# Two layers, Chebyshev attention beside an expert network: the attention output's transpose and projection move from the prefix sums' PSUM bank to a free quarter of the projection's bank

## What is computed

```python
xn = _layernorm(x, axis=-1)
qkv = jnp.einsum('bsd,ed->bse', xn, W_in)
xq = jnp.clip(q * inv_sqrt_d, -1.0 + EPS_CLAMP, 1.0 - EPS_CLAMP)
xk = jnp.clip(k * inv_sqrt_d, -1.0 + EPS_CLAMP, 1.0 - EPS_CLAMP)
Tq, Tk = _cheb(xq), _cheb(xk)                     # Chebyshev terms
kv_prefix = jnp.cumsum(Tk * v[:, :, :, None, :], axis=2)
ks_prefix = jnp.cumsum(Tk.sum(axis=-1), axis=2)
num = (Tq * kv_prefix * beta).sum(axis=3)
den = (Tq.sum(axis=-1) * ks_prefix * beta).sum(axis=3)
s = einsum(num / (den + EPS_DEN), W_out)
# beside it: a mixture of 8 experts, 2 per token
out = sum over e of cw_e * (gelu(xn @ w1[e].T + b1[e]) @ w2[e].T + b2[e])
x = x + s * silu(_layernorm(out + xn, ln_w, ln_b))
```

## Time and profile before

| what | value |
|---|---|
| median of 3 runs | 925.35 us (923.32 to 929.02) |
| profiled execution, its own time | 925.38 us |
| span in the profile | 923.5 us |
| mean granted TensorE clock | 0.849 of full |
| TensorE busy | 601.0 us (65%) |
| VectorE busy | 633.4 us (69%) |
| ScalarE busy | 449.1 us (49%) |
| GpSimd busy | 435.8 us (47%) |

### The profile page before, as it was taken

The page is one execution under the profiler, slowest core; times in us unless marked ns, Lnnn a source line. Parts: engine busy times, 40 slices in busy tenths (PEclk is TensorE's granted clock), DMA queues, the critical chain, the costliest instruction groups (busy, mean ns, idle before and its releaser), DMA issues.

```text
span 923.5 us, 21985 instructions
## 1 busy us (share of the span) xinstructions
PE 601.0 (65%) x7047; PEld 407.0 (44%) x7047; DVE 633.4 (69%) x1667; ACT 449.1 (49%) x1075; POOL 435.8 (47%) x697
## 2 busy tenths in 40 slices
PE   1888888888888888634542677667766776751220
PEld 0455555555555555422221455445544555520110
DVE  4587777777777777548671766776677667846667
ACT  1455555555555555313332676777677767610001
POOL 3145444444444444427774333333333333357783
PEclk9999999999999999856565888899889988955555
DMA  9910000000000000001113022222222222111221
GB/s 240 318 53 2 3 2 0 0 0 0 0 0 0 0 0 1 2 6 52 49 50 107 24 92 92 69 71 92 92 70 72 90 93 70 46 48 55 66 67 49
DMA packets 64526, 49.53 MB, mean 54 GB/s; under 512 B 10056, under 2 KB 55376, under 8 KB 64464
## 3 DMA queue, kind: packets, MB, share of 16 engines
q1 hardware_dynamic: 59328, 39.74, 13.8%
q0 software_dynamic: 5136, 9.02, 3.5%
HBM read 18.83 MB, written 18.35 MB: 40 GB/s over the span
## 4 chain that ended last, share of the span: by engine, by line
PE 34%; POOL 17%; issue 16%; ACT 15%; DVE 15%; DMA 2%; DVEq 1%; SPq 0%; POOLq 0%; ACTq 0%
POOL xbuf L528 7%; POOL experts_sb L541 7%; PE m_ps L986 6%; PE e_ps L998 5%; PE p_ps L869 4%; PE q_ps L899 2%; ACT xs L703 2%; PE y_ps L951 2%; ACT vd L603 2%; PE p_ps L943 2%; DVE x_all L1149 2%; ACT pexp L695 1%; DVE rot L1118 1%; ACT xs L608 1%; PE y_ps L832 1%
## 5 line engine op out<-in xcount | busy, mean ns | idle before, releaser
L576 ACT ACTIVATE pexp<-e_ps 128x512 f32<-128x512 f32 x128 | 76.4, 597 | 75.5 <-PE e_ps L816 73.8
L1260 DVE TENSOR_SCALAR early<-p_ps 128x256 f32<-128x256 f32 x32 | 13.6, 424 | 117.4 <-ACT vs L650 117.4
L986 PE MATMUL m_ps<-xs,wb 128*128 128x512 f16 x276 | 89.8, 442 | 2.1 <-ACT xs L703 1.3
L1085 DVE TENSOR_REDUCE mneg<-m_ps 128x4 bf16<-128x512 f32 x128 | 84.5, 681 | 4.6 <-PE m_ps L783 4.6
L528 POOL DMA_INDIRECT xbuf<-x,slots x64 | 65.9, 1030 | 33.6 <-issue 19.2
L958 PE MATMUL q_ps<-eye_sb,yn 128*128 128x128 f32 x32 | 11.5, 358 | 106.3 <-ACT early L671 75.5
L541 POOL DMA_INDIRECT experts_sb<-ybuf,slots x64 | 65.9, 1029 | 28.7 <-issue 18.5
L492 POOL COPY xs<-xs 128x128 f16<-128x128 f16 x32 | 12.8, 399 | 105.1 <-ACT xs L608 105.1
L603 ACT COPY vd<-p_ps 64x64 f32<-64x64 f32 x128 | 27.0, 211 | 71.8 <-DVE early L1120 69.4
L832 PE MATMUL y_ps<-pexp,vd 128*32 128x128 f32 x512 | 54.9, 283 | 2.8 <-ACT pexp L576 0.6
L1044 PE MATMUL e_ps<-b_sb,cwt 8*128 8x128 f32 x64 | 16.6, 436 | 61.7 <-ACT cwt L744 61.7
(11 more groups left out here) (218 smaller groups left out, 2124.2 us busy)
## 6 DMA issues: line engine op xcount, KB each, us to landing
wb<-experts_sb SPq DMA_DIRECT2D x46, 256.0 KB, 2.4
xbuf<-zero_sb SPq DMA_DIRECT2D x23, 256.0 KB, 4.0
xs<-xbuf SPq DMA_DIRECT2D x23, 256.0 KB, 2.9
ybuf<-rt SPq DMA_DIRECT2D x23, 256.0 KB, 2.5
experts_sb<-in_experts_w SPq DMA_DIRECT2D x8, 512.0 KB, 7.3
x_all<-in_x SPq DMA_DIRECT2D x8, 256.0 KB, 5.6
xbuf<-x,slots POOLq DMA_INDIRECT x64, 2.2
experts_sb<-ybuf,slots POOLq DMA_INDIRECT x64, 2.5
```

Source lines behind the costliest of these rows:

```text
L576: nc.scalar.activation(pexp[:, j, :, :], e_ps[j % 2][:, :, :], ACT.Exp, scale=float(D) ** -0.5).then_inc(exp_ready.sem, 1)
L986: last = nc.tensor.matmul(u_ps[f % 2], wb1[:, i % 2, f, a, :], xg16[:, i % 2, b, :], start=k == 0, stop=k == len(PARTS) - 1)
L1085: nc.vector.tensor_reduce(mneg[:, n.batch, j // 2, (j % 2) * NG:(j % 2) * NG + NG], m_ps[j % 2][:, :, :], AX.X, ALU.max, negate=True).then ...
```

## The change

`o_ps` becomes the fourth quarter of `p_ps`, the bank that `project` fills to three quarters. The waits follow the bank: the transpose no longer waits for the carry copies, but for the two readers of the projection (`v_copy` and `clip` of the chunk two ahead) and for the `s1_copy` of the chunk before; `sums` loses its wait on `s1_copy`, and `project` gets it. No instruction is added, removed or put elsewhere.

```diff
-        o_ps = cc_ps[1][:, 3 * P:4 * P]
+        o_ps = p_ps[:, 3 * C:4 * C]
...
                 after(pe, s_v_copied, c)
                 after(pe, s_clipped, c)
+                after(pe, s_s1_copied, c - 2)
                 nc.tensor.matmul(p_ps[:, 0:3 * C], xn1t_all[:, c, :], w_in[:, :], start=True, stop=True).then_inc(s_projected2, 1)
...
                 after(pe, s_carry_copied, min(c, NT - B))
-                after(pe, s_s1_copied, c)
                 nc.tensor.matmul(cc_ps[0][:, 0:3 * SW], tri_sb[:, :], kv[:, c % 2, 0:3 * SW], start=True, stop=True)
...
             def transpose_out(c):

                 pe.wait_ge(s_outs, CHEB2 * (c + 1))
-                pe.wait_ge(s_carry_copied, min(c + 1, NT - B))
+                pe.wait_ge(s_v_copied, min(c + 3, NT))
+                pe.wait_ge(s_clipped, min(c + 3, NT))
+                after(pe, s_s1_copied, c)
                 nc.tensor.transpose(o_ps, oc[:, :], eye_sb[:, :]).then_inc(s_oc_transposed, 1)
```

## The result

The changed kernel takes 883.57 us (median of 4 runs, 880.61 to 884.25) against 926.25 us of the kernel before (4 runs on the same chips, 923.32 to 929.02). The ratio is 0.9533, 95% interval 0.9496 to 0.9571: faster by 4.7%. The forecast was 883.0 us, range 871 to 896. The profiled execution took 883.1 us and has a span of 881.3 us.

What follows compares the result with a forecast made beforehand. The prediction took the main loop to be bound by a chain passing between engines, with the carry copies holding up TensorE's transpose. 925.4 less 21.2 (earlier transpose) less 21.2 (clock) gave 883.0 us, range 871 to 896.

Steps and rivals of the forecast that it cites:

- The bound: Main loop with expert passes: no engine full; a chain passing between engines sets the period, mean 13.21 us.
- ring: Loop's repeating chain: `rows_copy`, carry copies, transpose, up matmuls, third up group, its Gelu, ScalarE on to the next `rows_copy`.
- Part 1: Transpose in the loop no longer waits for carry copies: 1.01 us per iteration, 21 iterations, 21.2 us saved.
- Part 2: TensorE's clock in the loop: shorter split gaps remove 13 of 19 slow stretches, 1.63 us each, 21.2 us saved.
- Part 3: Transpose's new waits for `v_copy` and `clip` of the chunk two ahead, and an older `s1_copy`: cost nothing.
- Part 4: `s1_copy` wait moved from `sums` to `project`: met 1.4 us early there, nothing gained at `sums`; 0.
- Part 5: Before c = 8 and after c = 28, scatters, `yn` and gathers set the times: 0.
- Part 6: VectorE at the shorter period: carry add takes 1.75 us, ring 10.24 us still inside; cost 0, cover 0.51 us.
- rival B: VectorE becomes the loop's bound through a further meeting with GpSimd: 6 us back, 889 us; chance 0.08.
- A: TensorE's clock falls as often as before, in 19 of 21 iterations: 904.2 us; chance 0.10.
- C: Split gap before the up matmuls brings two slow stretches per iteration: 17 us more, 942 us; chance 0.02.
- D: Something ending just behind the carry copies holds the loop, so the change gains little: 925 us at most; chance 0.02.

Runs made afterwards that it cites:

- e1: Changed kernel with the transpose's old wait on the carry copies added again: 922.61 us, ratio 0.996.
- e9b: e3 with the last polynomial instruction moved behind `rows_copy` and, from c = 8 on, the carry copies behind `oc_copy`: 863.63 us, ratio 0.9326.
- e6: Changed kernel with one unused VectorE reduction ahead of each `clip` in the iterations with expert passes: 882.79 us, ratio 0.9535.
- e8: e3 with the three unused VectorE reductions of e7 added: 906.28 us on a slower chip, ratio 0.9460.
- e4: Kernel before the change with 12 unused matmuls in TensorE's idle time ahead of the transpose: 897.99 us, ratio 0.9699.
- e3: Changed kernel with 5 unused matmuls in TensorE's idle time ahead of the transpose: 873.05 us, ratio 0.9417.
- e2: Changed kernel with the wait on `s1_copy` kept at `sums` as well as at `project`: 887.94 us, ratio 0.9590.
- e7: Changed kernel with three unused VectorE reductions ahead of each `clip` in the iterations with expert passes: 883.71 us, ratio 0.9554.
- e5: Changed kernel with the transpose also waiting for `rows_copy`, making its idle time one piece: 889.46 us, ratio 0.9614.

## Why the prediction was right

**The bound** was read rightly: a ring, with the carry copies as one of its links (e1), running through ScalarE (e9b), and VectorE not on it (e6, e8). That everything else waits for the scatters between 406 and 497 us was too much said: VectorE is busy for 62.5 of these 91 us.

**Part 1** (21 x 1.01 = 21.2 us) measured 11.75 - 10.72 = 1.03 us per iteration, and 11.76 - 10.72 = 1.04 between e4 and e3: 21.6 us. That the trace of before held one iteration of the new kind, c = 29, gave this term to 2%. The thin cover of `oc_copy` held as well: in the changed kernel it ends at 728.27, and `project_out` starts at 728.56.

**Part 2** (the clock, 13 slow stretches fewer, 21.2 us) came out to the count: 6 of 21 are left. The price was 1.65 instead of 1.63 us (the mean of 13.38 had the shorter first period of 13.05 in it). The count was a choice between bounds of 0 and 19, and its exact hit is luck; e2, e6 and e7 had 7, e5 8. A seventh stretch, at c = 29, had not been counted and gave back 1.65 us. The page's rule that I set beside it (the Trainium skill, "TensorE: Matmul & The Clock Gate", section "HAM oscillation — how this bites in real kernels": keep the gaps short and the clock stays up) would have made it 873 us with gaps of 1.49 and 0.84 us. The trace disagrees: with those gaps 6 of the 21 iterations from c = 9 to c = 29 were slow, and of the split gaps only e3's 0.41 and 0.84 us left none behind c = 8. The direction is right, and no single gap length here divides fast from slow.

**Part 3** (the new waits of the transpose, 0): the transpose is released by `yn` throughout, with 0.84 us left to `rows_copy`.

**Part 4** (the moved `s1_copy` wait, 0): right for `project`, which starts 1.33 us after `s1_copy` (730.09 to 731.42). The statement that `sums` gains nothing was wrong by 0.1 us in the short iterations (e2): at c = 29 of the kernel before, `s1_copy` ended at 795.54, and I compared that with `project` alone. Keeping the wait at `sums` as well would have cost a part of the gain.

**Part 5** (nothing outside the loop): right as far as can be told. The change does act before the loop: from c = 1 to c = 6 the periods of the transpose are 8.1 to 9.0 instead of 9.3 to 9.8 us, and in e2, which keeps the wait of `sums`, 9.0 to 9.8. It gains nothing there, since TensorE then waits for the first expert rows of c = 7, 22.3 instead of 19.6 us. The 1.4 us by which c = 7 itself was earlier are within what executions differ by: in the changed kernel, e3, its repetition, e5, e6 and e7, which are the same up to there, it lies between 498.7 and 502.0 us.

**Part 6** (VectorE's longer carry add, hidden): as forecast. The add takes 1.8 us in the loop, in the slow iterations too, beside the earlier trace rows:

```profile
L1286 DVE TENSOR_TENSOR kv<-kv,early x28: 897/1827/1841, 448.3 to 763.4; 1x720 f32<-1x720 f32 x28
```

With 44.6 instead of 26.0 us in all it makes nearly all of VectorE's 19.3 us more of busy time, and it costs nothing. The exclusive lock of the Trainium skill ("SBUF — State Buffer", section "SBUF: two separate sides") agrees with these rows: 1.83 us where the add alone takes 0.90. The price put on rival B (a further meeting's overshoot goes in full into the period) was wrong in its kind, as e7 and e8 show: a later VectorE waits less for GpSimd.

**The sum.** Part 1 gave 21.6 and part 2 21.5 us, 43.1 together against 42.4 forecast. In the profiled executions 1.4 us before c = 7 come on top, and about 1.9 are given back behind c = 29, the seventh slow stretch among them, which leaves 42.6 against the 42.2 us of the spans. Both mechanisms are shown (e1, e3, e4). That the forecast time of 883.0 us lies so close to the measured 883.57 rests on the chosen count of six, and on rests outside the loop that nearly cancel.

**The rivals.** A (904 us) didn't happen, and e5 shows why: the idle time is shorter, and 19 slow stretches need the long gap. B, C and D didn't happen; no iteration had two slow stretches.

## What to carry to other kernels

When one engine runs a ring with a gap in it, look for an iteration at the edge of the loop that already lacks the wait in question: here its rows gave the new period within 0.03 us. Idle time on TensorE costs twice, once as time and once through its clock, so price a removed wait with both, and try cheap unneeded matmuls in the gap: here they brought 10 us on top of the change. An engine that waits in a long instruction for another can have more room than its idle rows show, as VectorE had here, and a chain of waits with an unexplained "issue" before an instruction may hide the real releaser. Adding work to the one suspected engine and taking 0.4 us out of the other told them apart here.

## What the runs showed of the hardware

- The share of slow iterations from c = 8 to c = 28 against TensorE's usual idle time per iteration: 3.5 us in one piece 19 of 21 (kernel before) and 17 of 21 (e1); 2.62 in one piece 8 of 21 (e5); 1.49 and 0.84 us 6 of 21 (changed kernel) and 7 of 21 (e2, e6); 0.41 and 0.84 us none but the first (e3); 0.95 us none (e4). The first, c = 8, has a longer idle time than the others in every kernel.
- Slow and fast iterations of one kernel differ by a fixed 1.64 to 1.66 us (1.55 in e2, whose short periods have the 0.1 us of the wait at the sums), with hardly anything between but the first period, c = 8.
- VectorE operations of 0.29 to 0.90 us grow to 1.13 to 1.84 us when they meet a GpSimd subtraction of 1.16 us, and which of them grows depends on when VectorE arrives.
- In the changed kernel the sums start 0.06 us after `s1_copy` has ended without waiting for it. With the wait kept they start 0.14 us after it, and each short period is 0.1 us longer (e2).
